# A recurrence, an attention block and four experts on one core: a small row tile taken ahead, and causal masks moved from TensorE to GpSimd

## The chip, the core and the metric

The kernel runs on one core of a Trainium2 chip. The metric is the device time of one execution in microseconds (us), the median of several executions; lower is better.

## The reference

x has 4 batches of 1024 time steps with 256 channels, all float32. Two blocks are added to it in turn. The first is a recurrence over time, the second attention followed by a mixture of four experts:

```python
h = layernorm(x)
px = h @ W_state.T + b_state
g = sigmoid(h @ W_gate.T + b_gate)
state = tanh(px[t] + state)            # 1024 steps, each [4, 256]
out[t] = g[t] * state
x = x + layernorm(out)

h = rms(layernorm(x)) * n1_w
q, k = rms(heads(h @ wq.T)), rms(heads(h @ wk.T))      # 16 heads of 16
attn = softmax(where(causal, q @ k.T / 4, -inf))
y = layernorm(x) + mask64(attn @ v @ wo.T)
xf = rms(y) * n2_w
wts = two best of softmax(xf @ gate_w.T), normed
y = y + mask64(sum_e wts[e] * expert_e(xf))            # e0, e1, e2 (four layers), e3
x = x + layernorm(y)
```

mask64 sets the first 64 of the 256 output channels to zero.

## The kernel before, in words

**Units.** Time is cut into 4 chunks of 256 steps (L14 to L18). A unit u is 256 rows that go through everything after the recurrence together; there are 16. In chunks 1 to 3 a unit is one batch's 256 steps; in chunk 0 a unit is 128 steps of two batches (`tiles_of_time`, L214), so that the first two units need only the first 128 steps of the recurrence.

**The head.** Eight tiles n of 512 rows (128 steps of all four batches). For each: load (`xin`), mean and variance of four row tiles and the inverse root by eight short operations on VectorE (`hst`, L1320 to L1309), scaling (`hsc`, L1382), transposes on TensorE (`htr`, L1045), a copy out of PSUM (`hcp`, L1389), the projections for the state and the gate (`hpx0`, `hpx1`, L1042, two groups of 4 matmuls of 512 columns each), the bias for the state on VectorE (`hout0`, L1403) and the tanh form of the gate on ScalarE (`hgt`, L938). Gates are stored to DRAM (`hsv`) and loaded again by unit (`gl`).

**The recurrence.** Step n is an add on GpSimd (`sadd`, L1703, 128x8 elements) and a tanh on ScalarE (`stanh`, L928). It runs beside everything else on those two engines. A unit starts with the product of its gates and states on VectorE (`pgate`, L1414, in chunk 0 L1418), which waits for the unit's last step.

**Attention.** Keys are the partition axis of a score block: `sc` (L1042, `PS<-QT,KT`) makes the scores of 128 keys against 256 queries for four heads with 4 matmuls; `ex` (L996) takes the exponential of 128x1024 elements on ScalarE; `av` multiplies by the values (`PS<-work,vlx`). Row maxima come from a first pass (`mxm`, L1502). Two blocks in each group of heads lie on the diagonal; in the second (r == 1) the first 128 queries see none of its keys, and `ex` and `av` already leave them out. Chunks 0 and 1 add the causal mask in PSUM by matmuls with a mask of large negative numbers (`PS<-maskk,identb`); chunks 2 and 3 set the masked exponentials to zero on GpSimd (`msk`, L1710, `affine_select`), and `av` waits for that.

**Experts and weights.** `up` and `dn` are the experts' layers. Twenty weight pieces are split into a high and a low part on VectorE (`wsh` L1337, `wsp` L1343) after the head, and stored; all experts' matmuls take the low parts from there.

**What sets the order.** Each engine has one static list. `arrange` (L249) writes every operation as an item with an engine, an assumed duration, a due time and what it waits for; `Plan.run` (L112) walks through time and gives each free engine the ready item with the smallest due time. `START` (a time for each unit) and `AT` (for each kind of work and chunk an offset from it) are those due times; `STAY` is what a change of tile mode or table adds to the score. The tables only set order: on the chip every engine takes its list in order and waits on semaphores.

## Time and profile before

| | us |
|---|---|
| median of 3 runs (1596.09 to 1600.81) | 1599.23 |
| the profiled execution | 1593.35 |
| its span, first to last instruction | 1591.6 |
| TensorE busy | 1407.8 |
| VectorE busy | 1093.4 |
| ScalarE busy | 970.3 |
| GpSimd busy | 295.7 |

The profile is of one execution. Busy time of TensorE overlaps with its weight loads (PEld). The mean granted clock of TensorE over the span is 0.936 of full speed. The recurrence runs from 23.5 to 842 us. A wait is put down to the instruction that released it.

### The profile page before, as it was taken

What the parts mean: (1) busy time and instruction counts of PE and PEld (TensorE: products, weight loads), DVE (VectorE), ACT (ScalarE), POOL (GpSimd) and SP (SyncE); (2) the same over time, 40 slices, a digit from 0 to 9 for tenths busy, and PEclk for the clock granted to TensorE, in tenths of its full rate; (3) what the DMA queues carried; (4) which work ended last, traced back from release to release, by engine and by line L of the source; (5) the groups of instructions that cost most, each with busy time, mean ns of one, the idle gap of its engine ahead of it and who ended that gap; (6) DMA issues with size and microseconds to landing.
All of it is one profiled execution on the core that took longest, in us unless ns stands there. A gap on an engine that the chain in (4) does not pass through costs nothing. (4 is left out here: it accounts for less than half of the span.)

```text
span 1591.6 us, 33801 instructions
## 1 busy us (share of the span) xinstructions
PE 1407.8 (88%) x12384; PEld 1114.6 (70%) x12384; DVE 1093.4 (69%) x2916; ACT 970.3 (61%) x2106; POOL 295.7 (19%) x1114
## 2 busy tenths in 40 slices
PE   6905778999997899999998899999999999999987
PEld 3404567889885578778876577877777568876787
DVE  7776586654668876758888776858896778574242
ACT  2545465765556677876564756387456875658941
POOL 3343332123323222223330100000000000000000
PEclk9956578999997999999999999999999999999999
DMA  5585436754575546636657555565656657565443
GB/s 171 146 283 154 112 105 186 214 156 144 182 217 183 166 156 180 201 108 210 199 178 216 153 181 165 186 205 174 205 180 189 204 168 216 162 207 172 134 122 109
DMA packets 244276, 278.54 MB, mean 175 GB/s; under 512 B 37136, under 2 KB 167696, under 8 KB 243856
## 3 DMA queue, kind: packets, MB, share of 16 engines
q1 hardware_dynamic: 244112, 276.39, 56.3%
q8 instruction: 99, 1.62, 0.4%
q14 instruction: 65, 0.53, 0.1%
HBM read 234.18 MB, written 43.45 MB: 174 GB/s over the span
## 5 line engine op out<-in xcount | busy, mean ns | idle before, releaser
L928 ACT ACTIVATE PX<-AD 128x8 f32<-128x8 f32 x1023 | 219.2, 214 | 228.8 <-POOL AD L1703 226.7
L1703 POOL TENSOR_TENSOR AD<-PX 128x8 f32<-128x8 f32 x1023 | 246.3, 241 | 585.5 <-ACT PX L928 569.8
L996 ACT ACTIVATE work<-PS 128x1024 f32<-128x1024 f32 (+1 forms) x312 | 288.1, 958 | 89.5 <-PE PS L1042 88.1
L1502 DVE TENSOR_REDUCE mx<-PS 128x2 f32<-128x1024 f32 (+3 forms) x256 | 256.3, 1020 | 76.1 <-PE PS L1042 75.6
L1042 PE MATMUL PS<-work,vlx 128*32 128x256 f32 (+2 forms) x2816 | 236.3, 377 | 20.8 <-ACT work L996 9.0
L1042 PE MATMUL PS<-EP,u_e_l 128*128 128x256 f32 x1024 | 201.7, 291 | 10.5 <-DVE EP L1368 8.2
L1042 PE MATMUL PS<-WB,work 128*128 128x192 f32 x1024 | 187.3, 338 | 8.2 <-ACT work L1021 3.9
L1042 PE MATMUL PS<-EP,WB 128*128 128x256 f32 x640 | 182.6, 285 | 0.0
L1042 PEld LDWEIGHTS PS<-WB,work 128*128 128x128 f32 x1024 | 171.2, 196 | 15.7 <-issue 9.1
L1042 PE MATMUL PS<-KT,QT 64*128 64x512 f32 (+3 forms) x768 | 151.2, 432 | 30.9 <-DVE mx L1502 11.4
L1042 PEld LDWEIGHTS PS<-EP,u_e_l 128*128 128x128 f32 x1024 | 165.7, 194 | 18.2 <-issue 13.7
L1021 ACT ACTIVATE work<-PS 128x512 f32<-128x512 f32 x176 | 104.3, 596 | 113.6 <-PE PS L1042 112.1
L1042 PE MATMUL PS<-XF,WB 128*128 128x256 f32 x576 | 163.2, 283 | 0.0
L1042 PEld LDWEIGHTS PS<-work,vlx 128*32 128x32 f32 (+1 forms) x2816 | 87.6, 114 | 106.7 <-issue 55.8
L1710 POOL TENSOR_SCALAR_AFFINE_SELECT work<-work 128x512 f32<-128x512 f32 x64 | 43.3, 689 | 632.5 <-ACT work L996 632.4
L1042 PE MATMUL PS<-QT,KT 64*128 64x256 f32 (+1 forms) x1344 | 141.9, 314 | 14.9 <-ACT work L996 7.1
L1042 PEld LDWEIGHTS PS<-QT,KT 64*128 64x128 f32 x1344 | 97.9, 190 | 67.6 <-issue 44.5
L1042 PEld LDWEIGHTS PS<-KT,QT 64*128 64x128 f32 x768 | 72.9, 197 | 79.1 <-issue 29.6
L1042 PEld LDWEIGHTS PS<-EP,WB 128*128 128x128 f32 x640 | 124.8, 195 | 0.1
L1632 DVE SCALAR_TENSOR_TENSOR UU<-PS,wts,UU 128x192 f32<-128x192 f32 x128 | 47.3, 411 | 103.7 <-PE PS L1042 103.5
L1502 DVE TENSOR_REDUCE mxb<-PS 128x2 f32<-128x256 f32 (+3 forms) x128 | 104.7, 818 | 17.8 <-PE PS L1042 17.4
L1042 PEld LDWEIGHTS PS<-XF,WB 128*128 128x128 f32 x576 | 110.9, 193 | 0.0
(170 smaller groups left out, 2393.6 us busy)
## 6 DMA issues: line engine op xcount, KB each, us to landing
KT<-ktd SPq DMA_DIRECT2D x112, 512.0 KB, 4.7
WB<-wlo_e_l SPq DMA_DIRECT2D x160, 256.0 KB, 3.0
WB<-wlo_e_up SPq DMA_DIRECT2D x64, 256.0 KB, 3.0
ktd<-KTs SPq DMA_DIRECT2D x128, 128.0 KB, 2.3
WB<-wlo_e_w SPq DMA_DIRECT2D x64, 256.0 KB, 3.0
WB<-wdn_e_down SPq DMA_DIRECT2D x64, 192.0 KB, 2.8
KT<-ktd SPq DMA_DIRECT2D x48, 256.0 KB, 3.7
KT<-ktd SPq DMA_DIRECT2D x32, 384.0 KB, 3.8
```

The source lines that it names most:

```text
L928: eng.activation(cur, AD[n % 2], ACT.Tanh).then_inc(of(*key), 1)
L996: eng.activation(pt[:, :, :, q0:L], two("sc", *a).rearrange("p a (l q) -> p a l q", l=2)[:, :, :, q0:L], ACT.Exp).then_inc(of(*key), 1)
L1021: eng.activation(half_of(hidden(u, name), h), one("up", u, name, h), ACT.Gelu).then_inc(of(*key), 1)
L1042: return eng.matmul(o, l, r, start=start, stop=stop, skip_group_check=skip)
L1502: eng.tensor_reduce(o, two("mxm", *a)[:, :, 0:w], AX, ALU.max, negate=True).then_inc(of(*key), 1)
L1632: ins = eng.scalar_tensor_tensor(U, ps[:, t, 0:NO], wts[:, u % 4, t, e_:e_ + 1], U, ALU.mult, ALU.add)
L1703: eng.tensor_tensor(AD[n % 2], PX[c % 2][:, :, :, t], PX[(n - 1) // L % 2][:, :, :, (n - 1) % L], ALU.add).then_inc(of(*key), 1)
L1710: eng.affine_select(out=p, in_=p, compare_op=ALU.is_ge, fill=0.0, base=0, pattern=[[0, 2], [0, 2], [1, 128]], channel_multiplier=-1).then_ ...
```

## The change

Four things change, and the two tables with them.

1. The first row tile of the head (the first 32 steps of all four batches, 128 rows) is loaded by four small DMAs (`xinf`), normalized, transposed, projected and given its bias on its own (`hstf`, `hscf`, `htrf`, `hcpf`, `hpxf`, `houtf`). The recurrence's first 32 steps wait for this tile alone. The rest of tile 0 (`xin 0`, also four DMAs, in the same order of rows) follows with 384 columns.
2. In chunk 1 the causal mask is no longer added by matmuls; GpSimd zeroes the exponentials, as in chunks 2 and 3.
3. In chunks 1 to 3 the scores of the second diagonal block are made for the last 128 queries only.
4. All of `START`, `AT` and `STAY` get other numbers, so every engine's list is in another order.

```diff
-STAY = {"pe": 16.7, "act": 8.9}
+STAY = {"pe": 21.2, "act": 6.4}
...
-START = (102.9, 140.3, 204.6, 251.3, 335.0, 429.5, 526.1, 598.9, 741.5, 802.0, 921.2, 978.2, 1089.0, 1179.7, 1287.1, 1381.6)
-AT = {"piece": (39.4, 44.9, 92.6, 23.9),
+START = (120.3, 168.9, 186.9, 253.4, 333.3, 420.3, 503.7, 595.0, 744.7, 804.3, 933.9, 996.5, 1104.9, 1196.9, 1299.3, 1387.8)
+AT = {"piece": (-41.3, 104.4, 54.7, 127.7),
...
-      "fin": (272.9, 230.9, 245.5, 366.3)}
+      "fin": (238.5, 93.3, 289.5, 553.3)}
...
+    add("sp", ("xinf",), 1.4, -20.0, lat=3.5)
+    add("dve", ("hstf",), 2.3, -20.0, ("xinf",))
+    add("dve", ("hscf",), 0.42, -20.0, ("hstf",))
+    add("pe", ("htrf",), 0.25, -20.0, ("hscf",), ("ident",), mode="128",
+        take={"P1": (("hcpf",),), "xnT": (("hpx0", 0), ("hpx1", 0))}, lat=DRAIN)
+    add("dve", ("hcpf",), dve(256), -20.0, ("htrf",))
+    add("pe", ("hpxf",), 0.9, -20.0, ("hcpf",), ("wl", "x0"), mode="128", take={"P1": (("houtf",),)}, lat=DRAIN)
+    add("dve", ("houtf",), 0.62, -20.0, ("hpxf",), ("wl", "bs"))
...
-        px = [("hout0", 2 * c + t // 128)] if c < 2 else [("pxl", c)]
+        px = [("houtf",)] if n < 32 else [("hout0", 2 * c + t // 128)] if c < 2 else [("pxl", c)]
...
-                mask = kb == u // 2 if c == 0 else r >= 0 and c < 2
-                add("pe", ("sc", u, g, kb), (0.236 if c else 0.45) + (0.5 if mask else 0), dg, ("kts", u, g, kb // 4), ("mtd", u),
+                mask = c == 0 and kb == u // 2
+                add("pe", ("sc", u, g, kb), (0.45 if c == 0 else 0.18 if r == 1 else 0.236) + (0.5 if mask else 0), dg, ("kts", u, g, kb // 4), ("mtd", u),
...
-                if r >= 0 and c >= 2:
+                if r >= 0 and c:
                     pt = ("msk", u, g, kb)
                     add("pool", pt, 0.75, dg, ("ex", u, g, kb))
...
+                elif kind == "xinf" or key == ("xin", 0):
+                    for b in range(B):
+                        x = A["L0_attn_x"][b, 0:128, :].rearrange("(i t) d -> t i d", t=32)
+                        i = slice(0, 1) if kind == "xinf" else slice(1, 4)
+                        eng.dma_start(half(0)[32 * b:32 * b + 32, i, :], x[:, i, :]).then_inc(of(*key), 16)
...
+                elif kind == "hpxf":
+                    pe.wait_ge(*done("wl", "x0"))
+                    pe.wait_ge(*done("hcpf"))
+                    for m in range(2):
+                        for kc in range(2):
+                            ins = mm(one(*key)[:, 128 * m:128 * m + 128], wx[:, kc, 128 * m:128 * m + 128], normed(0)[:, kc, 0:128],
+                                     kc == 0, kc == 1)
+                    ins.then_inc(of(*key), 1)
...
-                    ps, r = two(*key), kb - 2 * c
+                    ps, q0 = two(*key), 128 if c and kb == 2 * c + 1 else 0
...
-                                ins = mm(ps[:, par, 256 * pl:256 * pl + 256],
-                                         keys_of(kt, 2, n)[rows, pl, 128 * (kb % 4):128 * (kb % 4) + 128], qt[rows, 2 * g + pl, :],
-                                         pl == 0, True, True)
+                                ins = mm(ps[:, par, 256 * pl + q0:256 * pl + 256],
+                                         keys_of(kt, 2, n)[rows, pl, 128 * (kb % 4):128 * (kb % 4) + 128],
+                                         qt[rows, 2 * g + pl, q0:L], pl == 0, True, True)
...
-                    masked = [u // 2 == kb, u // 2 == kb] if c == 0 else [c == 1 and r == 0, c == 1 and r == 1]
-                    for i in range(2):
-                        for par in range(2) if masked[i] else ():
+                    for i in range(2) if c == 0 and u // 2 == kb else ():
+                        for par in range(2):
...
-                    pe.wait_ge(*done("msk" if r >= 0 and c >= 2 else "ex", *a))
+                    pe.wait_ge(*done("msk" if r >= 0 and c else "ex", *a))
...
+                    if n < 32:
+                        pool.wait_ge(*done("houtf"))
+                    elif c < 2:
                         pool.wait_ge(*done("hout0", 2 * c + t // 128))
```

In VectorE's list the four statistics of tile 0, its four scalings and the four statistics of tile 1 stood ahead of the first copy out of PSUM. Now it begins: statistics and scaling of the first small tile, the four statistics of tile 1, the small tile's copy (`hcpf`), three scalings of tile 1, the small tile's bias write (`houtf`), and then the other three statistics of tile 0. On the queue of SP the loads stand in the order `xinf`, `xin 0`, `xin 1`, `W_state`.

VectorE around the first unit's gate product, before (L1418; L1337 and L1343 are the halves of a weight piece's split, L1320 the statistics of the first unit):

```order
L1337 CAST u_e_l<-work 128x2x256
L1343 TENSOR_TENSOR WB<-work,u_e_l 128x512
L1418 SCALAR_TENSOR_TENSOR G<-G,PX 128x256 x2
L1337 CAST u_e_l<-work 128x2x256
L1343 TENSOR_TENSOR WB<-work,u_e_l 128x512
```

and now (L1484 is the gate product, L1469 the last bias write of the head, L1382 and L1388 the split):

```order
L1441 COPY work<-PS 128x1024
L1469 TENSOR_SCALAR work<-PS,bx 128x512 x2
L1484 SCALAR_TENSOR_TENSOR G<-G,PX 128x256 x2
L1382 CAST u_e_up<-work 128x2x256
L1388 TENSOR_TENSOR WB<-work,u_e_up 128x512
```

Twelve of the twenty weight pieces stood ahead of the first gate product; now none does, and all twenty come after it, five of them ahead of the first unit's statistics where there were four.

GpSimd's list, before (L1703 the adds of the recurrence, L1710 the masks of chunks 2 and 3):

```order
L1703 TENSOR_TENSOR AD<-PX 128x8 x999
L1710 AFFINE_SELECT work<-work 128x4x128
L1703 TENSOR_TENSOR AD<-PX 128x8 x10
L1710 AFFINE_SELECT work<-work 128x4x128
L1703 TENSOR_TENSOR AD<-PX 128x8 x14
```

and now (L1771 the adds, L1778 the masks), its first rows after the constants:

```order
L1771 TENSOR_TENSOR AD<-PX 128x8 x642
L1778 AFFINE_SELECT work<-work 128x4x128
L1771 TENSOR_TENSOR AD<-PX 128x8 x2
L1778 AFFINE_SELECT work<-work 128x4x128
L1771 TENSOR_TENSOR AD<-PX 128x8 x3
L1778 AFFINE_SELECT work<-work 128x4x128
L1771 TENSOR_TENSOR AD<-PX 128x8 x11
L1778 AFFINE_SELECT work<-work 128x4x128
```

The first mask stood behind 999 adds; now it stands behind 642, and 32 masks of chunk 1 lie between the adds of steps 642 and 851, singly, with 1 to 43 adds between two of them.

VectorE near the end, before (L1568, L1570 the end of the last unit's gate logits, L1320 to L1646 the normalization of unit 14, L1579 to L1609 the last unit's gate weights, L1368 the split of its first hidden layer):

```order
L1570 TENSOR_TENSOR gl<-gl 128x8
L1320 BN_STATS st<-UU 128x6 x2
L1323 BN_AGGR mv<-st 128x2 x2
...
L1643 TENSOR_SCALAR UU<-UU,mv,r 128x256 x2
L1646 TENSOR_TENSOR UU<-UU,XR 128x512
L1579 TENSOR_REDUCE gl<-gl 128x2
...
L1609 TENSOR_SCALAR wts<-wts 128x2
L1368 TENSOR_TENSOR EP<-work,EP 128x1024
```

and now (L1645 to L1675 the gate weights, L1698 the addition of a down projection of unit 14, L1413 the split, L1365 to L1712 the normalization):

```order
L1636 TENSOR_TENSOR gl<-gl 128x8
L1645 TENSOR_REDUCE gl<-gl 128x2
...
L1675 TENSOR_SCALAR wts<-wts 128x2
L1698 SCALAR_TENSOR_TENSOR UU<-PS,wts,UU 128x192 x2
L1413 TENSOR_TENSOR EP<-work,EP 128x1024
L1365 BN_STATS st<-UU 128x6 x2
...
L1709 TENSOR_SCALAR UU<-UU,mv,r 128x256 x2
L1712 TENSOR_TENSOR UU<-UU,XR 128x512
```

The normalization of unit 14 moved from ahead of the split to behind it, and an addition from before the gate logits to just ahead of it; on TensorE the down projection that it waits for now stands behind the first layer of the last unit.

## Rows read from the trace of the kernel before

**Rows 1.** Part 1 of the page: busy time, share of the span, instructions.
```profile
PE 1407.8 (88%) x12384; PEld 1114.6 (70%) x12384; DVE 1093.4 (69%) x2916; ACT 970.3 (61%) x2106; POOL 295.7 (19%) x1114
```
**Rows 2.** Windows: stretch and length, each engine's busy time, granted clock, DMA, GB/s.
```profile
80.00:280.00 200.00, 119.46 (x964) 98.48 (x963) 136.84 (x405) 102.52 (x365) 72.42 (x280) 0.67 0.55 168
...
480.00:720.00 240.00, 221.59 (x2076) 165.80 (x2077) 180.05 (x484) 174.97 (x435) 58.31 (x250) 0.95 0.53 164
...
842.00:1520.00 678.00, 640.49 (x6086) 484.79 (x6085) 472.00 (x1122) 442.22 (x540) 42.13 (x63) 0.99 0.58 182
```
**Rows 3.** Waits of TensorE, 80 to 280 us: total, times, longest.
```profile
PE PS L1045 <- DVE G L1418: 23.8, 3, 22.5
```
**Rows 4.** Timeline of the first 30 us: start, duration, instruction, idle before and releaser.
```profile
0.80 1.00 SPq L799 DMA_DIRECT2D UU<-in_L_attn_x  x2
...
4.73 1.40 DVE L1320 BATCH_NORM_STATS2 st<-UU 128x6 f32<-128x256 f32 x4 [4.73 <-DMA UU<-in_L_attn_x]
...
14.87 5.80 PE L1042 MATMUL PS<-work,vlx 128*128 128x512 f32 x8 [3.82 <-DVE work L1389]
...
20.52 1.04 PE L1045 MATMUL PS<-ident,UU 128*128 128x128 f32 x8
...
21.39 7.03 PE L1042 MATMUL PS<-work,vlx 128*128 128x512 f32 x16
...
22.04 1.40 DVE L1403 TENSOR_SCALAR PX<-PS,bx 128x512 f32<-128x512 f32 x2
...
23.48 0.22 ACT L925 ACTIVATE PX<-PX 128x8 f32<-128x8 f32 x1 [21.39 <-DVE PX L1403]
```
**Rows 5.** Windows of the recurrence alone (tile AD): tanhs and adds in a stretch.
```profile
24.00:30.00 6.00, 2.36 (x11) 2.34 (x11) 1.00 0.12 43
30.00:60.00 30.00, 11.21 (x52) 11.49 (x53) 1.00 0.56 157
```
**Rows 6.** Timeline, 83 to 103 us: the head's last gate tanhs, the first unit's start.
```profile
83.57 0.61 ACT L938 ACTIVATE work<-PS,bx 128x128 f32<-128x128 f32 x2
...
102.14 0.77 DVE L1418 SCALAR_TENSOR_TENSOR G<-G,PX 128x256 f32<-128x256 f32 x2
...
102.96 1.11 PE L1045 MATMUL PS<-ident,G 128*128 128x128 f32 x4 [22.50 <-DVE G L1418]
```
**Rows 7.** Timeline of TensorE, 503 us: a mask of chunk 1 and what follows.
```profile
503.26 0.40 PE L1042 MATMUL PS<-maskk,identb 128*128 128x256 bf16 x2
503.58 0.64 PE L1042 MATMUL PS<-work,vlx 128*32 128x256 f32 x8
```
**Rows 8.** Groups by line and form: score matmuls of 256 and of 128 columns.
```profile
L1042 PE MATMUL PS<-QT,KT 64*128 64x256 f32 x1152 | 124.3, 316 | 13.4 <-ACT work L996 7.1 <-DMA KT<-ktd 2.9 <-issue 1.3
...
L1042 PE MATMUL PS<-QT,KT 64*128 64x128 f32 x192 | 17.5, 307 | 1.5 <-DMA KT<-ktd 1.5
```
**Rows 9.** The masks of chunks 2 and 3 (line 1710): ns min/median/max.
```profile
L1710 POOL TENSOR_SCALAR_AFFINE_SELECT work<-work x64: 635/637/1192, 825.1 to 1515.0; 128x512 f32<-128x512 f32 x64
```
**Rows 10.** Timeline, 562 us: an exponential between two steps of the recurrence.
```profile
562.30 1.01 ACT L996 ACTIVATE work<-PS 128x1024 f32<-128x1024 f32 x1
562.49 0.21 POOL L1703 TENSOR_TENSOR AD<-PX 128x8 f32<-128x8 f32 x1 [1.75 <-ACT PX L928]
...
563.21 0.22 ACT L928 ACTIVATE PX<-AD 128x8 f32<-128x8 f32 x1
```
**Rows 11.** Timeline, 85 us: a weight piece on VectorE, an add on GpSimd beside it.
```profile
85.10 0.42 DVE L1337 CAST u_e_up<-work 128x512 fp32r<-128x512 f32 x1
...
85.56 0.69 DVE L1343 TENSOR_TENSOR WB<-work,u_e_up 128x512 fp32r<-128x512 f32 x1
85.56 0.75 POOL L1703 TENSOR_TENSOR AD<-PX 128x8 f32<-128x8 f32 x1 [0.33 <-ACT PX L928]
```
**Rows 12.** Timeline of TensorE at 1545 us, and the window from there.
```profile
1545.41 0.55 PE L1042 MATMUL PS<-EP,u_e_l 128*128 128x256 f32 x1 [4.08 <-DVE EP L1368]
...
1545.00:1550.00 5.00, 4.59 (x27) 4.62 (x28) 0.26 (x1) 0.08 (x1) 0.00 (x0) 0.67 0.01 3
```

More of the change, by code:

```diff
@@ new lines @@
+STAY = {"pe": 21.2, "act": 6.4}
+START = (120.3, 168.9, 186.9, 253.4, 333.3, 420.3, 503.7, 595.0, 744.7, 804.3, 933.9, 996.5, 1104.9, 1196.9, 1299.3, 1387.8)
+AT = {"piece": (-41.3, 104.4, 54.7, 127.7),
+      "post": (108.5, 29.1, -5.5, 37.9),
+      "prep": (-79.6, -11.3, -76.6, -46.8),
+      "value": (-215.6, 32.9, -128.0, -93.9),
+      "key": (-91.2, -92.6, 17.1, -86.2),
+      "query": (-68.6, 31.3, -84.5, -39.7),
+      "max": (-72.9, -65.0, -47.9, -52.7),
+      "maxima": (11.9, 24.3, 9.7, 30.5),
+      "bound": (84.1, -49.0, 83.1, 62.8),
+      "score": (6.4, 39.9, 18.3, 40.5),
+      "scores": (17.8, 2.9, 16.5, 10.5),
+      "av": (33.4, -31.3, 7.6, 1.0),
+      "merge": (37.5, -34.5, -5.3, -15.9),
+      "out": (-201.4, -15.7, -130.2, -131.7),
+      "gate": (-42.9, -114.7, -63.0, -0.1),
+      "l1": (21.0, 292.8, 148.7, 258.4),
+      "e0up": (155.5, 142.7, 23.6, 285.7),
+      "l2": (199.4, 270.7, 309.4, 375.3),
+      "e0dn": (289.6, 286.8, 465.8, -134.2),
+      "e1": (208.2, 248.7, 423.4, 216.2),
+      "l3": (220.1, 305.7, 171.8, 274.1),
+      "e3dn": (160.4, 294.0, 283.8, 302.6),
+      "e1dn": (263.8, 313.7, 290.7, 410.2),
+      "l4": (249.7, 319.9, 190.4, 359.0),
+      "e3up": (254.9, 261.6, 312.9, 335.1),
+      "e3out": (262.5, 269.8, 308.8, 387.5),
+      "fin": (238.5, 93.3, 289.5, 553.3)}
@@ L1054, in _ @@
                         pe.wait_ge(*x)
-                if kind == "htr":
+                if kind == "htrf":
+                    pe.wait_ge(*done("ident"))
+                    pe.wait_ge(*done("hscf"))
+                    for kc in range(2):
+                        ins = tr(one(*key)[:, 128 * kc:128 * kc + 128], half(0)[:, 0, 128 * kc:128 * kc + 128])
+                    ins.then_inc(of(*key), 1)
+                elif kind == "htr":
                     n, i = a
-                    ps = two("htr", n, 0)
+                    first = 0 if n else 1
+                    ps, col = two("htr", n, first), 128 * (i - first)
                     pe.wait_ge(*done("ident"))
@@ L1388, in _ @@
                     v.wait_ge(*done("htr", n, 3))
-                    eng.tensor_copy(xnT[place[("htr", n, 0), "xnT"]], two("htr", n, 0)).then_inc(of(*key), 1)
+                    eng.tensor_copy(normed(n), two("htr", n, 0)).then_inc(of(*key), 1)
+                elif kind == "houtf":
+                    v.wait_ge(*done("wl", "bs"))
+                    v.wait_ge(*done("hpxf"))
+                    for m in range(2):
+                        src = one("hpxf")[:, 128 * m:128 * m + 128].rearrange("p (b t) -> p b t", b=B)
+                        ins = eng.tensor_scalar(PX[0][:, m, :, 0:32], src, bx[:, m:m + 1], None, ALU.add)
+                    ins.then_inc(of(*key), 1)
+                elif key == ("hout0", 0):
+                    v.wait_ge(*done("wl", "bs"))
+                    v.wait_ge(*done("hpx0", 0))
+                    for m in range(2):
+                        dst = PX[0][:, m, :, 32:128].rearrange("p b (i t) -> p b i t", t=32)
+                        ins = eng.tensor_scalar(dst, by_batch(two("hpx0", 0)[:, m, 0:384]), bx[:, m:m + 1], None, ALU.add)
+                    ins.then_inc(of(*key), 1)
                 elif kind == "hout0":
```

96 lines of the change are left out of this document (46 added, 50 removed).

## The prediction, made before the changed kernel had run

> **What bounds the kernel now.** I began with the page's busy shares: TensorE is busy for 88% of the span, no other engine for over 70% [rows 1]. The stretches in windows tell where the missing 12% are [rows 2]. From 80 to 280 us TensorE works for only 119.5 of 200 us, at a mean granted clock of 0.67, so partly at the lower of its two levels; from 480 to 720 it works for 221.6 of 240, and from 842 to 1520 for 640.5 of 678. So there is a ramp with 80 us of idle TensorE, and a body that is nearly full. In the ramp the waits of TensorE name the cause: the gate product of the first units (L1418), 23.8 us, the largest of them [rows 3]. The gate product waits for the recurrence: the first unit's ran at 102.14, its transposes on TensorE at 102.96 after 22.5 us of idleness [rows 6], and the 128th step ended just ahead of it. The recurrence in turn starts at 23.48, behind the whole first head tile [rows 4]. So two things end the time: when the recurrence has done 128 (then 256, then 512) steps, and how much work TensorE has after that.
>
> **The sum is made against the profiled execution, 1593.35 us (span 1591.6).** The median shown is 1599.23, 5.9 above it; I subtract from the median what I subtract from the profile. Two times of this kernel can be told apart at 0.3%, some 4.8 us.
>
> **Term 1: the recurrence starts earlier, about -8 us.** Before, statistics of four row tiles start at 4.73, a 512-column projection of 5.80 us starts at 14.87, the bias write at 22.04, the first tanh at 23.48 [rows 4]. Now one tile of 128 rows goes ahead. Step by step: two DMAs take 1.00 us to issue [rows 4], so four end at 2.8 and the small loads land near 4.5 to 5; statistics of one tile plus the same eight short operations, 2.3; scaling, 0.4: near 7.5. But the order puts the statistics of tile 1 (3.75) ahead of the copy of the head, and its load is issued behind eight small ones, at 4.8; with the 3.9 us that the first load took from issue to use it lands at 8.7. So: 8.7 + 3.75, copy 0.4, projection of a quarter of 5.80, hidden partly, bias write half of 1.40: first tanh near 15.2, 8.3 us earlier. The rest of tile 0 is projected by about 25 and written by 30; step 32 is reached at 15.2 + 32 x 0.53 = 32 (11 steps in 6 us when nothing interferes [rows 5]), so no new stall. The other 95 steps, at 30/52 = 0.58 to 0.6 us, reach 128 at 88 to 89. The head's own end is the other bound: TensorE begins its bulk at 22 instead of 15, has 2.6 + 3 x 3.5 + 6 x (7.03 + 1.04) = 61.5 us of it [rows 4], ends at 83.5 instead of 80.5, the last gate tanhs end 3.7 later as now (80.56 to 84.2, [rows 6] has their last), and their save must land, at most 3.9: 91. The first unit can so start at 91 instead of 103, 12 earlier. Not all of it is kept: the order has no weight piece ahead of the first gate product where it had 12, so 12 pieces of 0.42 + 0.69 us [rows 11], 13.4 us of VectorE, now lie among the first units' operations, and their DMAs among those of the keys on the queue of SP, which waits for each piece. VectorE has 63 us of idle time in this ramp [rows 2], but the chain through it is serial; I put a third of 13.4 on it, 4. Bounds: -12 (all hidden) and 0 (12 lost of 12).
>
> **Term 2: 32 masks leave TensorE, -9 us.** A masked score block of chunk 1 has two mask matmuls that hold TensorE from 503.26 to 503.58, 0.32 us [rows 7]; 32 blocks give 10.2. What GpSimd takes instead is 32 x 0.637 = 20.4 us [rows 9], between steps 642 and 851 of the recurrence. There ScalarE does an exponential of 1.01 us between two steps: it starts at 562.30, the add of the step runs from 562.49 to 562.70, and the next tanh starts at 563.21, as the exponential ends [rows 10]. A mask of 0.64 us that starts with the exponential's end holds the add behind that tanh from 563.5 to 563.9, 0.4 us, and what ScalarE does between that tanh and the next (another exponential, or a copy) hides most of it. I give back 1 us of 10.2. Bounds: -10.2 to +10 (0.64 each on the path, 20.4, less 10.2). Step 767, which the first unit of chunk 2 needs, has 22 masks ahead of it and may slip by 22 x 0.64 = 14 us, less the 8 of term 1. Expert work of the units before stands there for TensorE, so I count nothing; without that cover it would be 6 us.
>
> **Term 3: narrower scores, -3 us.** 48 blocks (the second diagonal block of chunks 1 to 3) have 4 matmuls of 128 columns instead of 256. The form with 256 costs 124.3/1152 = 0.108 us, that with 128 in chunk 0 costs 17.5/192 = 0.091 [rows 8]: 192 x 0.017 = 3.3. Bounds: 0, and half of 192 x 0.108, 10.4.
>
> **Term 4: the order of the last unit, -5.5 us.** TensorE stands still for 4.08 us before 1545.41, waiting for a subtraction on VectorE that is queued behind the previous unit's final normalisation and the gate weights; then the clock is 0.67 over 5 us, 1.6 us of lost work [rows 12]. In the new order the normalisation comes after the subtraction, and TensorE has a down projection (L1698 is its addition) and the other expert's first layer in between. Both go. Bounds: -5.7 and 0, if the down projection's own addition, now ahead of the subtraction, comes late.
>
> **Term 5: all other places of the rewritten tables, 0 with 12 us to either side.** From 842 to 1520 TensorE idles 37 us in small pieces [rows 2]; every one can shrink or grow, and the trace of before cannot say which. ScalarE changes its table 119 times instead of 129 by my count of the order, 10 x 1.28 us less on an engine that is not the bound.
>
> Sum: -8 - 9 - 3.3 - 5.5 = -25.8. Profile 1567.6, median **1573.4 us**.
>
> A rule of the Trainium skill bears on term 2. The row first: an add of the recurrence that takes 0.20 us alone took 0.75 beside a VectorE subtraction of 0.69 us with two inputs in SBUF [rows 11]. "GPSIMD Engine Reference", section 1, says that the SBUF interfaces of GpSimd are shared with VectorE, with contention where VectorE runs a two-port mode or has two SBUF inputs. The trace agrees; by that rule the masks themselves can be held, which is rival D.
>
> **The rivals.**
> A, slower: the masks hold up the loop of tanh and add, and through it ScalarE. GpSimd takes its list in order, so the add behind a mask waits for it; ScalarE in its order waits for the add, the exponentials behind it with it, and TensorE for these. Place: 505 to 707 us. Price, if each mask takes its longest time in the trace, 1.19 us [rows 9], and all of it shows: 32 x 1.19 = 38 us against a gain of 26: 1611. It decides, as slower, from (25.8 + 4.8)/32 = 0.96 us a mask. For it: the trace has no mask between adds in this stretch, and TensorE has only 18.4 us of slack there. Against it: in the order of ScalarE the exponential stands directly ahead of the tanh whose add follows the mask, so GpSimd never waits for an exponential that the tanh would not have waited for anyway, and most of a mask lies beside other work of ScalarE. Chance 0.05.
> B: the early start is not kept (late loads of the head tile, or all 12 us lost among the weight pieces): term 1 is 0, 1581. That the recurrence does not start earlier at all, because the statistics of tile 1 wait for a load that lands at 15 instead of 9, is in it. Chance 0.15.
> C: the new tables fill TensorE's idle time of the body better than the old: a third of the 18.4 + 37.5 us that stand idle in the two stretches of [rows 2]: 1573 - 19 = 1554. For it: fewer table changes; against it: nothing in the trace. Chance 0.13.
> D: the shared port. The longest mask took 1.19 us instead of 0.64 [rows 9], and VectorE is busy for 180 of 240 us where the new masks run [rows 2]: 32 x 0.55 = 17.6 us more in the loop of recurrence and exponentials: 1591. Against it: the mean of the 64 masks in the trace is 0.69, taken at the same load of VectorE. Chance 0.05.
>
> **How the numbers follow.** Forecast 0.62, A 0.05, B 0.15, C 0.13, D 0.05. The range has to leave out A's upper part and the far half of C: 1557 to 1593, about 0.84. Faster than 1594.4: nearly all of the forecast, B, C, half of D and little of A, 0.87; within 0.3%, 0.06; slower than 1604, most of A and the tail of term 5, 0.07.
>
> **What would show it.** Right: first tanh near 15 us, first gate product near 89 to 91, the first key maxima 6 to 10 us earlier; TensorE's mask matmuls 64 instead of 128, and its busy time down by 12 to 14 us; POOL with 96 selects, none of the first 32 followed by a long wait of ScalarE; no idle time of 4 us near the end. Wrong: more idle TensorE from 480 to 720 than the 18.4 us of now (A or D), the ramp's idle time still at 80 us (B), or a body stretch whose idle time differs by over 12 us from now (term 5).

## The result, and the profile of the changed kernel

The changed kernel takes 1606.09 us (median of 16 runs, 1600.63 to 1614.37) against 1599.03 (16 runs, 1593.49 to 1602.85): 1.0052 times the time before, 95% interval 1.0035 to 1.0069. It is slower by 8.3 us where 25.8 less was forecast, and lies outside the range. The profiled execution took 1601.77 us, span 1600.0, 8.4 more than that of before, so its trace can be held against the rows of before; both profiled executions are among the fastest of their kernel. One run of the kernel before, beside the first four experiments, took 1661.37 us at a granted clock of 0.81, a slower state of the chip, and is in no comparison.

Part 1 of the page, to be read beside [rows 1]:

```profile
PE 1405.1 (88%) x12328; PEld 1112.7 (70%) x12328; DVE 1098.1 (69%) x2927; ACT 959.4 (60%) x2096; POOL 314.2 (20%) x1146
```

TensorE should have lost 10.2 us (masks) and 3.3 us (narrower scores) of busy time, and has lost 2.7. Its groups by form say where the rest is (for each: busy, mean ns | idle time before). The masks fell from 24.1 us (x128) by 13.1, the scores rose from 124.3 + 17.5 [rows 8] to 146.1 though they stream fewer columns, and the products with the values rose from 144.1 to 148.1 with the same count:

```profile
L1070 PE MATMUL PS<-maskk,identb 128*128 128x256 bf16 x64 | 11.0, 301 | 0.0
...
L1070 PE MATMUL PS<-QT,KT 64*128 64x256 f32 x960 | 109.2, 327 | 16.4 <-ACT work L1024 5.8 <-issue 5.8 <-DMA KT<-ktd 2.5
...
L1070 PE MATMUL PS<-QT,KT 64*128 64x128 f32 x384 | 36.9, 294 | 7.9 <-DMA QT<-MT 3.9 <-ACT work L1024 1.8 <-DMA KT<-ktd 1.6
...
L1070 PE MATMUL PS<-work,vlx 128*32 128x256 f32 x1920 | 148.1, 407 | 7.1 <-ACT work L1024 3.8 <-POOL work L1778 2.6 <-DVE mx L1568 0.3
```

In the kernel before, masks and products were:

```profile
L1042 PE MATMUL PS<-maskk,identb 128*128 128x256 bf16 x128 | 24.1, 295 | 0.0
...
L1042 PE MATMUL PS<-work,vlx 128*32 128x256 f32 x1920 | 144.1, 395 | 13.1 <-ACT work L996 8.1 <-POOL work L1710 4.4 <-DVE work L1530 0.5
```

The windows, against [rows 2]:

```profile
80.00:280.00 200.00, 124.18 (x972) 98.83 (x971) 134.34 (x397) 102.91 (x359) 67.76 (x264) 0.73 0.58 173
480.00:720.00 240.00, 213.54 (x1953) 161.60 (x1951) 180.15 (x477) 164.37 (x418) 76.01 (x277) 0.91 0.53 160
842.00:1520.00 678.00, 638.72 (x6042) 482.74 (x6043) 474.94 (x1128) 435.51 (x551) 44.36 (x82) 0.98 0.58 182
```

From 480 to 720 us TensorE is idle for 26.5 us instead of 18.4, and its granted clock is 0.91 instead of 0.95. Over the whole span it is idle for 194.9 us (1600.0 - 1405.1) instead of 183.8. So the freed work became idle time, and more work than before ran at the lower level of the clock: from 480 to 720 us 37.5 us of TensorE's busy time lie at that level, before 18.1 (over the whole span 147.3 and 129.6).

**Where the 8.4 us are lost.** I count the columns that TensorE has streamed, without masks and scores, and ask how much later the changed kernel has done what the kernel before had done at a given time. It is 1.6 us behind at 280, 3.2 at 480, 12.4 at 720, 14.3 at 1520 and 8.4 at the end. The largest part, 9 us, is lost from 480 to 720. By the waits of TensorE in this window (in all, times, longest) it is not lost at the masks, for which it waits 0.5 us, but at a load and at waits to which the trace gives no releaser; the longest wait of the kernel before in this window was 2.4 us:

```profile
PE PS L1070 <- issue: 8.7, 3, 4.1
PE PS L1070 <- DMA WB<-wlo_e_down: 5.2, 1, 5.2
...
PE PS L1070 <- POOL work L1778: 0.5, 1, 0.5
```

**The head and the first unit.** The timeline (start, duration, instruction, idle before and what ended it):

```profile
15.09 0.22 ACT L951 ACTIVATE PX<-PX 128x8 f32<-128x8 f32 x1 [13.01 <-DVE PX L1447]
...
92.31 0.77 DVE L1484 SCALAR_TENSOR_TENSOR G<-G,PX 128x256 f32<-128x256 f32 x2 [3.16 <-ACT PX L954]
...
99.32 1.09 PE L1073 MATMUL PS<-ident,G 128*128 128x128 f32 x4 [8.27 <-DMA gd<-work]
111.08 1.12 PE L1073 MATMUL PS<-ident,HA 128*128 128x128 f32 x4 [10.67 <-DVE HA L1528]
...
161.00 0.69 DVE L1388 TENSOR_TENSOR WB<-work,u_e_up 128x512 fp32r<-128x512 f32 x1
```

The first tanh starts at 15.09 (forecast 15.2), the gate product at 92.31 (before 102.14, [rows 6]). But its transposes wait 8.27 us for the last gate save, and start at 99.32, 3.6 us earlier than before (102.96): 6.2 of the 9.8 us are gone here. The first transposes of queries and keys (L1172) are still 3.6 us earlier (133.04, before 136.68), the fourth, with pieces between them on VectorE, 0.5 (145.18, before 145.66). The last weight piece is split at 161.00; before it was at 121. The key bound of unit 0, one operation on VectorE, starts at 173.7 us in the kernel before and at 179.1 now:

```profile
L1577 DVE TENSOR_SCALAR MT<-PS x1: 412/412/412, 179.1 to 179.1; 16x256 fp32r<-16x256 f32 x1
```

So the key bound comes 5.4 us later, not 8 earlier. The last 5 us are lost in one place. VectorE stands still for 9.50 us at a weight piece whose load was issued at 153.70, behind six loads of keys, and the first row maxima (L1568) stand behind this piece in its list; they start at 159.28, before at 154.56:

```profile
158.94 0.43 DVE L1382 CAST u_e_up<-work 128x512 fp32r<-128x512 f32 x1 [9.50 <-DMA work<-in_L_ffn_e_up]
159.28 0.75 DVE L1568 TENSOR_REDUCE mx<-PS 128x2 f32<-128x256 f32 x2
```

The three other kernels in the new order show the same wait, 9.0 to 9.2 us.

**The recurrence.** Step 127 ends 9.6 us ahead of before, step 255 is 5.0 behind, 511 is 6.4 ahead, 767 is 15.8 behind (621.4 to 637.2), 1023 is 17.9 behind. Four single steps (207, 589, 763 and 769) take 7.9, 9.0, 8.7 and 4.9 us, and step 344 takes 5.1; the longest step of the kernel before takes 5.0. In each of the four ScalarE stands at an operation that waits for TensorE, with the next tanh behind it in its list. The timeline of ScalarE:

```profile
156.37 0.60 ACT L992 ACTIVATE QKB<-PS 128x512 f32<-128x512 f32 x1 [6.70 <-PE PS L1070]
...
467.06 0.60 ACT L1049 ACTIVATE work<-PS 128x512 f32<-128x512 f32 x1 [8.25 <-PE PS L1070]
467.56 0.21 ACT L954 ACTIVATE PX<-AD 128x8 f32<-128x8 f32 x1
...
630.09 1.28 ACT L1049 ACT_TABLE_LOAD   x1 [6.67 <-PE PS L1070]
...
637.20 0.21 ACT L954 ACTIVATE PX<-AD 128x8 f32<-128x8 f32 x1
...
642.26 0.60 ACT L1024 ACTIVATE work<-PS 128x512 f32<-128x512 f32 x1 [4.23 <-PE PS L1070]
```

and TensorE, ahead of the first three, at loads that had not landed:

```profile
152.39 0.47 PE L1070 MATMUL PS<-KT,QT 64*128 64x128 f32 x2 [6.41 <-DMA KT<-ktd]
...
462.27 0.55 PE L1070 MATMUL PS<-EP,u_e_l 128*128 128x256 f32 x1 [6.40 <-DMA WB<-wlo_e_l]
...
627.09 0.55 PE L1070 MATMUL PS<-XF,u_e_down 128*128 128x256 f32 x1 [5.21 <-DMA WB<-wlo_e_down]
```

**The tail.** From the residual addition of unit 15 to the end of its last operation it is 58.5 us (1538.83 to 1597.37), before 63.1 (1525.85 to 1588.92): 4.5 less.

```profile
1538.83 0.56 DVE L1603 TENSOR_TENSOR UU<-UU,PS 128x384 f32<-128x384 f32 x1 [0.55 <-PE PS L1070]
...
1596.68 0.69 DVE L1712 TENSOR_TENSOR UU<-UU,XR 128x512 f32<-128x512 f32 x1
```

### The profile page after: what moved, and what is told of

Its sections match the earlier page's. It is cut to its first block, busy times and chain, and to the rows that moved or that the text cites. A ratio compares the mean times of both kernels' runs of the same rounds, so it can differ in the third digit from the quotient of the medians.

```text
span 1600.0 us, 33743 instructions
## 1 busy us (share of the span) xinstructions
PE 1405.1 (88%) x12328; PEld 1112.7 (70%) x12328; DVE 1098.1 (69%) x2927; ACT 959.4 (60%) x2096; POOL 314.2 (20%) x1146
## 4 chain that ended last, share of the span: by engine, by line
PE 64%; DVE 12%; ACT 8%; DMA 5%; issue 5%; SPq 3%; POOL 2%; ACTq 0%; DVEq 0%; POOLq 0%
PE PS L1070 60%; DVE mx L1568 3%; ACT work L1024 3%; PE PS L1073 2%; PE PS L1172 2%; POOL AD L1771 2%; ACT PX L954 2%; DMA KT<-ktd 1%; SPq L876 1%; DMA UU<-in_L_attn_x 1%; DVE st L1365 1%; DMA ktd<-KTs 1%; ACT L1024 1%; DVE mxb L1568 1%; DMA WB<-wlo_e_l 1%
## 5 line engine op out<-in xcount | busy, mean ns | idle before, releaser
L1771 POOL TENSOR_TENSOR AD<-PX 128x8 f32<-128x8 f32 x1023 | 246.3, 241 | 555.6 <-ACT PX L954 548.3
L1568 DVE TENSOR_REDUCE mx<-PS 128x2 f32<-128x1024 f32 (+3 forms) x256 | 255.4, 1019 | 74.6 <-PE PS L1070 74.0
L1070 PE MATMUL PS<-work,vlx 128*32 128x256 f32 (+3 forms) x2824 | 243.3, 386 | 21.6 <-ACT work L1024 6.3
L1778 POOL TENSOR_SCALAR_AFFINE_SELECT work<-work 128x512 f32<-128x512 f32 x96 | 63.0, 664 | 654.8 <-ACT work L1024 654.5
L1070 PEld LDWEIGHTS PS<-work,vlx 128*32 128x32 f32 (+1 forms) x2824 | 91.8, 117 | 106.9 <-issue 60.9
L1568 DVE TENSOR_REDUCE mxb<-PS 128x2 f32<-128x256 f32 (+3 forms) x128 | 104.7, 818 | 7.5 <-PE PS L1070 7.4
L1698 DVE SCALAR_TENSOR_TENSOR UU<-PS,wts,UU 128x192 f32<-128x192 f32 x128 | 47.3, 411 | 87.8 <-PE PS L1070 87.7
```

The source lines that it names most:

```text
L1070: return eng.matmul(o, l, r, start=start, stop=stop, skip_group_check=skip)
L1568: eng.tensor_reduce(o, two("mxm", *a)[:, :, 0:w], AX, ALU.max, negate=True).then_inc(of(*key), 1)
L1698: ins = eng.scalar_tensor_tensor(U, ps[:, t, 0:NO], wts[:, u % 4, t, e_:e_ + 1], U, ALU.mult, ALU.add)
L1771: eng.tensor_tensor(AD[n % 2], PX[c % 2][:, :, :, t], PX[(n - 1) // L % 2][:, :, :, (n - 1) % L], ALU.add).then_inc(of(*key), 1)
L1778: eng.affine_select(out=p, in_=p, compare_op=ALU.is_ge, fill=0.0, base=0, pattern=[[0, 2], [0, 2], [1, 128]], channel_multiplier=-1).then_ ...
```

## The experiments

The change has parts (head tile, masks, narrower scores) and new lists. "The new order" below is the changed kernel's; "the old order" is that of the kernel before, with a part put in by hand. Times are medians of 6 to 12 runs; differences in us are the ratio less 1 times 1600, with the 95% interval, always against the kernel before on the same chip; where they differ by some us from the difference of the medians, the interval covers both.

### Masks in the new order: left out, and on TensorE

```diff
-                    pe.wait_ge(*done("msk" if r >= 0 and c else "ex", *a))
+                    pe.wait_ge(*done("msk" if r >= 0 and c >= 2 else "ex", *a))
```

with the 32 selects taken out of GpSimd's list; the second run puts the mask matmuls back into the scores besides.

> The changed kernel in its own order on every engine, but the 32 masks of chunk 1 are left out altogether: GpSimd does not run them, TensorE neither, and the products with the values follow the exponentials directly (so the future keys of chunk 1 are not masked). Theory H (holds): the time went where ScalarE stands in its order behind an operation whose input from TensorE is late (the steps of the recurrence that take 7.9, 9.0, 8.7 and 4.9 us, ending at 157.6, 467.8, 632.1 and 643.0 us), which no mask causes; leaving the masks out gives 0 to 4 us: 1602 to 1606. Theory M (masks): the masks in the loop of tanh and add cost what was lost from 480 to 720 us, some 15 us; then this is at 1588 to 1592.

> The changed kernel in its own order, but the 32 masks of chunk 1 are mask matmuls on TensorE again and none is on GpSimd. Theory H: TensorE has 32 x 0.32 = 10.2 us more to do and the holds stay: 6 to 10 us above the changed kernel, 1612 to 1616. Theory M: 15 us come back and 10 are paid, 1600 or less.

Measured: without masks 1612.69, +10.6 [6.6, 14.7]; on TensorE 1611.26, +11.7 [7.2, 16.2]; the changed kernel itself +8.3 [5.6, 11.0]. The three can't be told apart. Without masks the gain is none (theory M falls), and 10.2 us of matmuls more on TensorE cost nothing that can be measured against that, where theory H had expected 6 to 10 (the intervals, each some 4 us to either side, leave room for a cost of a few us). Both theories took TensorE for the bound of chunk 1. In the trace with masks on TensorE it is busy for 219.24 of the 240 us from 480 on, without them for 214.73 at a lower clock:

```profile
480.00:720.00 240.00, 219.24 (x1977) 162.95 (x1976) 173.69 (x469) 160.63 (x409) 53.30 (x241) 0.91 0.53 157
```

```profile
480.00:720.00 240.00, 214.73 (x1896) 162.34 (x1896) 174.22 (x464) 159.32 (x412) 54.91 (x245) 0.89 0.54 160
```

Counted in columns as above, these two kernels (masks on TensorE, no masks) lose 14.5 and 16.2 us from 480 to 720. The changed kernel loses 9.2, and the two below that change only the tail of the old order lose 1.2 and 2.8, which is the scatter of single traces. TensorE waits in both for what it waits for in the changed kernel: 9.1 and 9.9 us without a releaser, 2.9 and 5.6 for the load of `wlo_e_down`. So by these traces the loss in this stretch belongs to what the three kernels share, the new order above all, and not to the place of the masks.

### The parts in the old order

```diff
+                    if e in self.forced and k[0] != "stanh" and k != self.forced[e][self.at[e]]:
+                        continue
...
+    P.forced = arrange_plain()
```

`arrange_plain` is the old `arrange` with its tables; the lists of TensorE, VectorE, the DMA queue and, but for the tanhs, ScalarE are taken from it. The tanhs get new places: 217 of them in the first run and, with the head tile, 1021 of 1024 in the second.

> The kernel before with its old tables and, on TensorE, VectorE and the DMA queue, its old order; only the masks of chunk 1 move to GpSimd (put into its list when their exponentials are due) and the 48 second diagonal blocks are scored 128 queries wide; the tanhs are placed anew among ScalarE's other work, which keeps its order. Theory H: terms 2 and 3 of the forecast by themselves, -9 and -3: 1587, at most 1593. Theory M: masks cost in the loop, over 1600.

> As the run before it, and the head tile of the changed kernel too, in the old order: its operations go ahead of everything on VectorE, TensorE and the DMA queue, all other operations stay as in the kernel before. First tanh near 10 to 12 us. Theory H: the edits are worth what was forecast once the order is one that the chip has been seen to keep: -8 to -12 more than the run before it, 1575 to 1581. Rival P (the parts themselves): the head tile or the masks do not pay in any order, 1595 or more.

Measured: 1613.32, +12.2 [8.0, 16.2], and 1617.79, +19.2 [14.4, 24.0]. With both parts the order that was known to run well gets slower; theory H falls. That the parts themselves cost (P) these two runs don't show, since the tanhs moved with them. The waits of TensorE from 480 to 720 us with the masks on GpSimd (in all, times, longest):

```profile
PE PS L1306 <- POOL work L1973: 6.5, 10, 1.5
PE PS L1306 <- ACT work L1260: 6.0, 8, 1.4
PE PS L1309 <- DVE work L1780: 4.1, 3, 3.0
```

The first line is new. In the second run, with the head tile, 128 steps are done at 86.6 us, yet the gate product runs at 107.82, since 12 weight pieces stand ahead of it on VectorE and begin at 89.58 us, when the head is done, instead of 84.03:

```profile
107.21 0.69 DVE L1661 TENSOR_TENSOR WB<-work,u_e_l 128x512 fp32r<-128x512 f32 x1
107.82 0.75 DVE L1757 SCALAR_TENSOR_TENSOR G<-G,PX 128x256 f32<-128x256 f32 x2
```

### What a mask and a narrow score are worth on TensorE

The kernel before, every list unchanged:

```diff
-                    masked = [u // 2 == kb, u // 2 == kb] if c == 0 else [c == 1 and r == 0, c == 1 and r == 1]
+                    masked = [u // 2 == kb, u // 2 == kb] if c == 0 else [False, False]
```

and, in the other, `qt[rows, 2 * g + pl, q0:L]` with `q0` 128 in the second diagonal block.

> The kernel before with its order unchanged on every engine; the 64 mask matmuls of chunk 1 are left out and nothing takes their place (the future keys of chunk 1 are not masked). It prices what TensorE gains when the masks leave it, without anything on GpSimd. Theory F (as forecast: TensorE bounds chunk 1): 32 x 0.32 = 10.2 us faster, 1589 to 1591. Theory C (chain: in the second half of chunk 1 TensorE waits for exponentials and maxima often enough that its freed time turns into idle time): 0 to 4 us faster, 1596 to 1600; then the +12 of the run with the masks on GpSimd in the old order is their wait in the list of GpSimd and nothing comes back from TensorE.

> The kernel before with its order unchanged; only the 48 second diagonal score blocks are 128 queries wide. Forecast term 3 by itself: -3.3, 1597. Rival: nothing, since these matmuls stand ahead of exponentials that TensorE waits for: 1600.

Measured: 1596.93, -0.6 [-4.2, 2.9], and 1599.38, +0.5 [-3.2, 4.2]. Theory C and the rival: neither gives anything that can be measured, though 10.2 us of matmuls are gone in the first; by the interval it gains at most 4. Its profiled execution was the fastest of its 12, 1587.39, and is by the count of columns 5 us faster from 480 to 720; the medians don't keep that. The windows from 480 to 720 (before: 221.59, x2076, clock 0.95 [rows 2]) don't decide it: a stretch fixed in time fills up with the work that follows, and without 64 mask matmuls there are only 20 fewer in it:

```profile
480.00:720.00 240.00, 220.36 (x2056) 169.31 (x2057) 182.03 (x495) 178.25 (x448) 59.96 (x259) 0.94 0.57 169
```

```profile
480.00:720.00 240.00, 221.45 (x2055) 165.17 (x2054) 177.65 (x477) 172.35 (x424) 57.42 (x246) 0.93 0.54 162
```

### The four long steps

The new order; on ScalarE 12, 5, 12 and 4 tanhs taken ahead of the operations that waited.

```diff
+    for key, first, n in ((("qkc", 1, 1), 207, 12), (("gel", 3, "e2_l2", 1), 569, 5), (("gel", 3, "e2_l3", 0), 589, 12), (("gel", 4, "e3_down", 0), 763, 4)):
+        order = P.order["act"]
+        ahead = [("stanh", t) for t in range(first, first + n)]
+        order[:] = [k for k in order if k not in ahead]
+        i = order.index(key)
+        order[i:i] = ahead
```

> The changed kernel with its order, but on ScalarE 12, 5, 12 and 4 tanhs of the recurrence are taken ahead of the four operations that stood waiting for TensorE (before steps 207, 569, 589 and 763). Theory H (the holds of the recurrence cost time): 767 steps are done 8 to 14 us earlier and the end comes 5 to 10 us earlier than in the changed kernel, 1597 to 1602. Theory T (the transfers that TensorE waited for are the loss, and the recurrence is a bystander, since TensorE's order is fixed): the recurrence is earlier, the end within 3 us of the changed kernel's 1606.

Measured: 1612.41, +14.1 [10.9, 17.1]: not faster than the changed kernel, likely some us slower. Theory H falls in this form. The long steps only moved: now step 223 takes 10.1 us, 601 takes 12.5, 767 takes 12.7, and step 767 ends at 646.8 instead of 637.4. Fewer tanhs were left to lie between the operations behind. Whether the long steps of the new order cost time in themselves is not settled by this run; that moving these tanhs does not cure them is.

### The head tile and the weight pieces

The old order, the head tile alone, the pieces placed where they come due (`100.0 + i`), the gate product ahead of them; then the same with the subtraction of a piece on 2 columns (the high part is stored in place of the low one).

```diff
-                    eng.tensor_tensor(lo, WS[a[0]], plain(hi), ALU.subtract).then_inc(of(*key), 1)
+                    eng.tensor_tensor(lo[:, :, 0:2], WS[a[0]][:, :, 0:2], plain(hi[:, :, 0:2]), ALU.subtract).then_inc(of(*key), 1)
```

> The kernel before, in its old order, with the head tile alone (masks on TensorE, scores wide); the weight pieces on VectorE and the DMA queue are taken out of that order and put where they come due, the first gate product ahead of them. First tanh near 11 us, 128 steps near 87, first gate product 88 to 95. Theory W (weight pieces): before, 12 pieces of 1.33 us lay in VectorE's idle time ahead of the first gate product, and an earlier start only puts them into the first unit's chain: the key bounds of unit 0 end at 172 to 180 as in the kernel before (174.1), and the whole is 1597 to 1606. Theory F (forecast, term 1): unit 0's bounds end 8 us earlier, the whole at 1592.

> As the run with the head tile alone and spread pieces, but the second operation of each of the 22 weight pieces on VectorE (0.69 us, the low part) works on 2 columns of 256 and the high part is stored in its place (so the low parts of the expert weights are not what the reference has): some 22 x 0.5 = 11 us of VectorE less among the first units. Theory W (the pieces ate the early start): unit 0's key bounds end 5 to 9 us earlier than with full pieces (176.8), 168 to 172, and the whole at 1603 to 1609. Rival: VectorE's load is not what holds the chain of the first unit: within 3 us of 1613.7.

Measured: 1613.75, +15.8 [12.6, 18.9], and 1609.4, +9.8 [6.2, 13.1]. Gate product and key bound of unit 0: 102.1 and 173.7 before; 87 and 176.3 with full pieces; 86 and 173.8 with light ones:

```profile
L1852 DVE TENSOR_SCALAR MT<-PS x1: 412/412/412, 176.3 to 176.3; 16x256 fp32r<-16x256 f32 x1
```

```profile
L1852 DVE TENSOR_SCALAR MT<-PS x1: 412/412/412, 173.8 to 173.8; 16x256 fp32r<-16x256 f32 x1
```

Theory W holds in kind: 15 us of earlier start are gone by the first key bound. The pieces' second operation is worth 2.5 us there, less than the 5 to 9 expected; and in the nine kernels that leave the ramp as it was, the bound lies anywhere from 171.1 to 174.6, so 2.5 us of one trace each is barely a difference (in the kernels of the new order it lies from 179.1 to 181.9). A piece also occupies the DMA queue and waits for its load, which this run leaves in. And most of the 15.8 us is lost behind the ramp, at a recurrence that is 36 us ahead at step 767. The tanhs had been placed anew there too (1008 of them). The head tile with the tanhs in their old places was not tried, so what it costs or gives by itself stays open.

### GpSimd's list, or the tanhs' places on ScalarE

The edit of the first of these runs, three idle selects for a mask:

```diff
+                    if u < 2 * B:
...
+                        for i in range(3):
+                            x = scratch[:, 2 * i:2 * i + 2]
+                            ins = eng.affine_select(out=x, in_=x, compare_op=ALU.is_ge, fill=0.0, base=0, pattern=[[1, 2]],
+                                                    channel_multiplier=-1)
```

The expectation says that the scores are narrow too. They are not: the kernel that ran has the wide ones (1152 matmuls of 256 columns).

> As the run with the masks on GpSimd in the old order (scores narrow too), with the same places in the lists, but each of the 32 masks of chunk 1 is three selects of 2 elements on a scratch tile, some 0.2 us each, and the products with the values do not wait for them (the future keys of chunk 1 are not masked). It parts the two ways in which a mask on GpSimd can cost. Theory G (GpSimd's list: the adds of the recurrence behind the masks come late, with them the tanhs and all that stands behind these on ScalarE): the cost stays, 1607 to 1613. Theory V (the product with the values waits for the mask, 6.5 us of TensorE's time shown, and the clock falls with it): the cost goes, 1597 to 1602.

> The kernel before with every list kept but GpSimd's: the 32 masks of chunk 1 are selects there, each behind the add that comes before its exponential's end, and the 48 narrow scores are in it; ScalarE's list is word for word the old one, the tanhs' places too. Theory G (a select in GpSimd's list costs): 1607 to 1613, as with tanhs placed anew. Theory P (places of the tanhs on ScalarE): the cost goes, 1597 to 1602.

> The kernel before, its masks on TensorE and its scores wide; only in ScalarE's list the tanhs from step 661 to 1019 stand where the run with the masks on GpSimd had them (217 of them, by up to 6 other operations later or earlier). Theory G: nothing, 1597 to 1602, or some us where tanhs come later than they could. Theory P: the whole cost by itself, 1607 to 1613.

| old order, with | tanhs on ScalarE | difference, us |
|---|---|---|
| masks left out | old places | -0.6 [-4.2, 2.9] |
| narrow scores | old places | +0.5 [-3.2, 4.2] |
| masks on GpSimd, narrow | old places | +5.6 [2.4, 8.8] |
| nothing else | anew, steps 661 to 1019 | +9.1 [5.6, 12.5] |
| masks on GpSimd, narrow | anew | +12.2 [8.0, 16.2] |
| idle selects, wide | anew | +11.4 [7.0, 15.8] |

The places of 217 tanhs, moved past at most 6 operations and with no other change, cost 9.1 us: theory P for the larger part. (162 of them stand earlier than before, 55 later.) The masks on GpSimd, with narrow scores, cost 5.6; TensorE waits for them 6.9 us between 540 and 842 us, where it had waited for none:

```profile
PE PS L1306 <- POOL work L1973: 6.9, 9, 1.5
```

Idle selects in their place cost as much as the masks when the tanhs are placed anew, but the new places alone explain that; so it does not decide between the theories that it was made for. Where the 9.1 us go can't be read well from its trace: the profiled execution was the fastest of 12 (1601.81), and shows the gate product of the first unit of chunk 2 5.7 us later (627.57, before 621.88) and the rest of the loss in small pieces.

### The tail

```diff
+    for engine, key, behind in (("dve", ("fin", 14), ("gll", 15, "e2_l1")), ("sp", ("ost", 14), ("wr", 15, "e1_w1", 1, 0))):
+        order = P.order[engine]
+        order.remove(key)
+        order.insert(order.index(behind) + 1, key)
```

The first run moves the normalisation of units 1 and 14 on VectorE alone, the second that of unit 14 and its store on the DMA queue; the edit shown is the second's.

> The kernel before; on VectorE alone two operations change places with the one behind them: the final normalisation of units 1 and 14 goes behind the subtraction of the next unit's first hidden layer (line L1368 of the kernel before), for which TensorE stood still 3.39 us before 386.31 and 4.08 us before 1545.41. If both waits are on the path: 4.08 + 1.6 of clock + 3.39, at most 9 us, likely 5 to 8: 1591 to 1594. If time freed at 386 is lost again behind it, as the runs before this one suggest for the body, only the tail's 4 to 5.5 are kept: 1594 to 1595.

> The kernel before; on VectorE the final normalisation of unit 14 behind the subtraction of unit 15's first hidden layer, and on the DMA queue its store behind the loads of two weight pieces of unit 15 (in the run before it, which left the store in its place, the load behind the store came late and TensorE stood still 4.07 us before 1554.38 in place of 4.08 before 1545.41). If the wait and the clock behind it are the path of the tail: 4 to 5.5 us faster than before, 1594 to 1596; rival: the tail is bounded by something behind it, 1599.

Measured: 1596.4, -4.2 [-7.4, -1.0], and 1594.12, -3.5 [-6.2, -1.0]: both faster than both kernels, by little, and not to be told apart. In the first the 3.39 us at 386 are freed, unit 2 ends 4.7 us earlier, and unit 5's residual addition runs at the same 605.0 us as before: all given back within 220 us. Its tail shows the wait of [rows 12] turned into another, because the store of unit 14, now later, stands ahead of a weight load in the queue. TensorE, then the queue:

```profile
1554.38 5.46 PE L1047 MATMUL PS<-WB,work 128*128 128x192 f32 x16 [4.07 <-issue]
```

```profile
1551.18 0.39 SPq L912 DMA_DIRECT2D out<-UU  x1
1551.61 0.47 SPq L799 DMA_DIRECT2D WB<-wdn_e_down  x1
```

With the store moved too, the wait for the load is gone; what is left of the 4.08 us (0.79, as in the first run), and the first matmul behind it at 0.36 us where it took 0.55 [rows 12]:

```profile
1548.14 0.36 PE L1047 MATMUL PS<-EP,u_e_l 128*128 128x256 f32 x1 [0.79 <-DVE EP L1373]
```

From unit 15's residual addition to the end it is 56.5 us instead of 62.5 by the ends of the two operations, 6.0 less. That moving the store is worth time is seen in the trace alone.

## Why the prediction was wrong

**Term 1 (-8), wrong by about 13.** The first tanh (15.2 forecast, 15.09) and the gate product (91 forecast, 92.3) were right. The step that failed is "12 pieces ... 13.4 us of VectorE, now lie among the first units' operations ... I put a third of 13.4 on it, 4". From the gate product to the key bound of unit 0 it was 71.6 us and is 86.8: 15.2 more. The kernel before did the pieces in a time in which VectorE could do nothing else; an earlier gate product doesn't remove them, it takes away their cover. The save's landing, which I had put at 91, was also late: the transposes waited for it until 99.3. The traces of the two kernels divide the 15.2 us: 6.2 ahead of these transposes, 3.1 among the pieces between the transposes of queries and keys, and 5.2 from the fourth of these to the first maxima, which stood behind the piece whose load landed late; the last 0.7 lie behind them. So the piece's price is for the larger part its place on the queue and its wait, which I had named without a price. No run took these waits away, so this division is read and not tested. By TensorE's work the ramp costs less, 1.6 us at 280 and 3.2 at 480.

**Term 2 (-9), wrong, and for the reason I had taken as given.** The arithmetic was right, 10.2 us of matmuls; the sentence that fails is the first, "a body that is nearly full", from which it followed that less work is less time. Leaving the masks out, in the old order and in the new, gave nothing that can be measured. And the price on GpSimd, "I give back 1 us", is 5.6 us in the old order (with narrow scores); in the new order TensorE waits 0.5 us for masks from 480 to 720, and leaving them out brings nothing back. Rival A named that mechanism but priced it by the length of a mask; TensorE waits for the mask itself, up to 1.5 us at a time, at products that the old order had placed for an exponential alone. Step 767 came 15.8 us late, close to the 14 that I allowed for the masks ahead of it (21 by the trace, not 22); without them on GpSimd it came 24.7 and 17.6 late, so this closeness is chance.

**Term 3 (-3.3): 0** (+0.5, from -3.2 to 4.2, alone in the old order). Same reason. In the trace the two forms take 4.3 us more than before, not 3.3 less; the wide one takes 327 ns in the mean instead of 316, with more of TensorE's time at the lower clock.

**Term 4 (-5.5): right.** 4.5 in the changed kernel, 6.0 of the trace and 3.5 of the median when it is the only edit.

**Term 5 (0, 12 to either side): about +7.** It is what is left of 8.4 after +5.4 (ramp), 0, 0 and -4.5; with the ramp at 3.2, by TensorE's work, it is 9.7. The size lies in what I had allowed, but the step failed that put it at 0 because the trace of before could not say more. Most of it is lost from 480 to 720 us, where TensorE waits 5.2 us for a load and 8.7 without a releaser; it is lost there without masks too. I had seen the tables as rearranging TensorE's small gaps. The runs show one cause that I had not priced: where the tanhs of steps 661 to 1019 stand in ScalarE's list is worth 9 us in the old order, and the new lists move nearly all of them. How much of the loss in the changed kernel is theirs, and how much is that of loads placed later on the queue, is not shown; the new tables without the head tile were not run.

**The rivals.** A, as mechanism, is part of the truth, at a seventh of its price. B is right in its effect ("all 12 us lost among the weight pieces") and was given 0.15; alone it would have given 1581. My sign for A or D, more than 18.4 us of idle TensorE from 480 to 720, came true (26.5) with neither: without any mask on GpSimd it is 25.3. C did not happen. D fell: with VectorE as busy as in [rows 2], the 96 selects took 634/640/1024 ns (least, median, longest).

```profile
L1778 POOL TENSOR_SCALAR_AFFINE_SELECT work<-work x96: 634/640/1024, 504.9 to 1525.9; 128x512 f32<-128x512 f32 x96
```

Nine of the 96 took over 0.7 us, three of them in chunk 1, and together 2.3 us more than the median. The Trainium skill ("GPSIMD Engine Reference", section 1) says that GpSimd shares its SBUF interfaces with VectorE, with contention where an instruction of VectorE has two SBUF inputs. The trace agrees: each of the nine ran beside such an instruction, the longest, 1024 ns, beside a gate product. It also shows that the contention is rare and not certain: a select beside the addition `UU<-UU,XR` at 512 us took 638 ns. No case had all the larger parts of the gain fail together. Terms 2 and 3 rested on one assumption, so they failed together, and term 5 was given a width but no cause that could fill it; the chance of 0.87 for faster was far too high.

## What to carry to other kernels

A busy share of 90% in a stretch does not say that less work there gives less time: leave the work out altogether and time that, before paying for a place to move it to. In a kernel whose lists are fixed beforehand for five engines, a serial loop threaded through two of them makes every list depend on its pace; price an earlier start by what had used the wait, and an edit by whether it leaves the loop's places alone. When an operation goes later on one engine, look at its store on the queue too. To find where a kernel falls behind, ask when it has done the same work, not how busy a stretch is.

## What was not expected of the hardware

- The granted clock fell in the stretch in which idle time grew. With 13.5 us less to do, TensorE was busy for only 2.7 us less; the same 1920 products took 407 ns in the mean instead of 395. The mean clock from 480 to 720 us was 0.95 before, 0.91 in the changed kernel and 0.89 to 0.94 in the fourteen kernels of the experiments, one trace each.
- A select of 2 elements on GpSimd takes 195 ns in the mean, an add of 8 elements 243, a select of 512 elements 640 (median): the part that does not grow with the size is most of a small one.

```profile
L1982 POOL TENSOR_SCALAR_AFFINE_SELECT scratch<-scratch 128x2 f32<-128x2 f32 x96 | 16.1, 195 | 23.7 <-ACT work L1262 23.7
```

- Executions of one kernel differ by up to 1% (the kernel before: 1591.3 to 1606.5 beside the experiments), the size of the effects here. Two profiled executions of nearly the same lists differ by up to 7 us in places (unit 11 ends at 1257.4 in the kernel before and at 1264.8 with only the tail changed), so single traces settle no cause of that size; the medians of 6 to 12 runs do, to 3 or 4 us.
